# Four masked graph layers on one core: the attention-head stage splits the next quad's scores in two halves, one graph apart

## The chip, the cores and the metric

The kernel runs on one core of one Trainium2 chip. The metric is the device time of one execution in microseconds (us), lower is better; the median of three runs stands for a kernel.

## The reference

64 graphs of 128 nodes with 128 features pass four layers, each behind a layer norm and a ReLU and each added to its input. The change touches only the third, an attention with 8 heads:

```python
h = input @ W                                   # per graph: 128 nodes x 128 features
s1 = einsum('bif,hf->bhi', h, a1); s2 = einsum('bjf,hf->bhj', h, a2)
e = leaky_relu(s1[:, :, :, None] + s2[:, :, None, :] + a_b[None, :, None, None])
att = softmax(where(adj[:, None, :, :] > 0, e, NEG_INF), axis=-1)
h_prime = einsum('bhij,bjf->bif', att, h) / 8   # mean over the 8 heads
```

## The kernel before

The four layers are four stages, one after the other; the whole of `x` stays in on-chip memory. The stage of the heads (`phase_heads`) runs from about 640 to 960 us. It works on 16 quads of 4 graphs. Each engine runs an instruction list of its own, and every quad is cut into four **slots**, `i` = 0 to 3, one per graph. The slots are a software pipeline: in the slot of graph n the engines work on graphs n to n-4. Semaphores order the engines; the order within an engine is that of the code. The first quad and the last four stand written out, the others run in a loop of two quads per turn (`graphs`).

For graph n the work goes as follows. A slot number is that in which the step is issued, counted from the graph's own slot.

- TensorE, slot 0: four matmuls write the masked scores of 8 heads to `psE` (L955, L957). ScalarE copies them with a ReLU (L1018), also in slot 0.
- VectorE, slot 1: finishes the leaky ReLU in `eu` (L1068) and takes the maximum per head (L1072, "the maximum").
- ScalarE, slot 2: eight exponentials (L1012), which need that maximum.
- VectorE, slot 3: the reciprocal of the sums (L1059). GpSimd, slot 3: scales the exponentials by it (L918). TensorE, slot 3: 16 instructions of L977 turn and add up the heads in `psA`.
- VectorE, slot 4: copies `psA` to `attT` (L1064). TensorE, slot 4: multiplies by `h` (L965).

On VectorE one slot is therefore the reciprocal L1059, the copy L1064, then L1068 and L1072. On TensorE it is the scores L955/L957, L965, one job for the next quad, and L977.

The jobs for the next quad g+1 are spread over the slots of quad g. In slot 0 TensorE turns the inputs (L935) and ScalarE applies the ReLU (L996). In slot 1 TensorE forms the small score rows in `psF` (L940), and VectorE, behind that slot's maximum, splits them into three bf16 parts (`split_scores`): L1035 writes part 0, L1037 the rest in float32, L1040 part 1, L1042 part 2. SyncE waits for L1042 (L894), sends the parts to DRAM with two DMAs (L896), waits for both, and fetches them back in another layout with two DMAs (`lhs` at L900, `rhs` at L901). The semaphore `placed` tells TensorE that they are there; it waits for it ahead of L955 in slot 0 of quad g+1. In slot 3 TensorE writes `h` of quad g+1 over `psF` (L945), once L1037 is done, and ScalarE copies it (L1001). In slot 3 VectorE also adds the finished quad to `x` (L1047) and takes its layer-norm statistics (L264).

Of the kernel before, what the change touches and what calls it, by code (L numbers as in the profile page):

```python
# [40 lines left out]
def done(n):  # L41
    return n + 1 + BIAS
# [218 lines left out]
def ln_stats(nc, k, g):  # L261

    for i in range(G):
        nc.vector.bn_stats(k.stats[:, bass.ds(g * G + i, 1), :], k.x[:, bass.ds((g * G + i) * C, C)])  # L264
# [575 lines left out]
def phase_heads(nc, k):  # L840
# [6 lines left out]
    with ExitStack() as ctx:  # L847
# [26 lines left out]
        def graphs(eng, slot):  # L874


            def quad(g, p, first=False, tail=False, left=2):
                for i in range(G):
                    slot(g, p, i, lambda lag: (not first or i >= lag) and (not tail or i < lag), lambda l: l <= left)
            quad(0, 0, first=True)  # L880
            with eng.Fori(0, QUADS // 2 - 2) as t:
                for u in (0, 1):
                    quad(2 * t + (u + 1), 1 - u)
            quad(QUADS - 3, 1)
            quad(QUADS - 2, 0, left=1)
            quad(QUADS - 1, 1, left=0)
            quad(QUADS, 0, tail=True, left=0)

        with nc.Block() as block:
            @block.sync  # L890
            def _(sp):
                for g in range(QUADS):
                    p = g % 2
                    sp.wait_ge(s_split, done(4 * g + 3))  # L894
                    for half, first in ((0, 0), (1, S2)):
                        sp.dma_start(bounce[p, half].rearrange("t h c -> h t c"), parts[first:first + HEADS, p, :, :]).then_inc(bounced, 16)  # L896
                    sp.wait_ge(bounced, 32 * (g + 1))
                    if g >= 2:
                        sp.wait_ge(e_mm, done(g * G - (G + 1)))
                    sp.dma_start(lhs[0:ROWS, p, :], bounce[p, 0].rearrange("t h c -> (t h) c")).then_inc(placed, 16)  # L900
                    sp.dma_start(rhs[ROWS:KR, p, :, :], bounce[p, 1]).then_inc(placed, 16)  # L901
                    sp.wait_ge(placed, 32 * (g + 1))
# [124 lines left out]
            @block.vector  # L1027
            def _(dve):
                for s in (s_split, leaky, negmax, recip, att_ready, added):
                    dve.sem_inc(s, BIAS)  # L1030
                def split_scores(g, p, placed_before=True):
                    dve.wait_ge(s_mm, done(g))
                    if placed_before:
                        dve.wait_ge(placed, 32 * g - 32)
                    nc.vector.tensor_scalar(parts[:, p, 0, :], psF[0:SR, :], ab[:, 0:1], None, ALU.add).then_inc(s_split, 1)  # L1035
                    dve.wait_ge(s_split, done(4 * g))
                    nc.vector.scalar_tensor_tensor(out=rest[:, :], in0=psF[0:SR, :], scalar=ab[:, 0:1], in1=parts[:, p, 0, :],  # L1037
                                                   op0=ALU.add, op1=ALU.subtract).then_inc(s_split, 1)
                    dve.wait_ge(s_split, done(4 * g + 1))
                    nc.vector.tensor_copy(parts[:, p, 1, :], rest[:, :]).then_inc(s_split, 1)  # L1040
                    dve.wait_ge(s_split, done(4 * g + 2))
                    nc.vector.tensor_tensor(parts[:, p, 2, :], rest[:, :], parts[:, p, 1, :], ALU.subtract).then_inc(s_split, 1)  # L1042

                def finish(g):
                    dve.wait_ge(out_mm, done(g * G + (G - 1)))
                    xs = k.x[:, bass.ds(g * QC, QC)]
                    nc.vector.tensor_tensor(xs, psO[:, :], xs, ALU.add).then_inc(added, 1)  # L1047
                    dve.wait_ge(added, done(g))
                    ln_stats(nc, k, g)

                def slot(g, p, i, behind, ahead):
                    n = g * G + i
                    odd, even = (i - 1) % 2, i % 2
                    if behind(3):
                        m = n - 3
                        dve.wait_ge(expd, done(m))
                        at = (i - 3) % G
                        dve.wait_ge(scaled, done(m - G))
                        nc.vector.reciprocal(rz[:, at, :], zs[:, at, :]).then_inc(recip, 1)  # L1059
                    if behind(4):  # L1060
                        m = n - 4
                        dve.wait_ge(att_mm, done(m))
                        dve.wait_ge(out_mm, done(m - 2))
                        nc.vector.tensor_scalar(attT[:, even, :], psA[:, 0:N], 1.0 / HEADS, None, ALU.mult).then_inc(att_ready, 1)  # L1064
                    if behind(1):
                        m = n - 1
                        dve.wait_ge(e_copied, done(m))
                        nc.vector.scalar_tensor_tensor(out=eu[:, odd, :], in0=psE[:, odd, :], scalar=0.01, in1=eu[:, odd, :],  # L1068
                                                       op0=ALU.mult, op1=ALU.add).then_inc(leaky, 1)
                        dve.wait_ge(leaky, done(m))  # L1070
                        dve.wait_ge(expd, done(m - 2))
                        nc.vector.tensor_reduce(nmx[:, odd, :], eu[:, odd, :].rearrange("n (h j) -> n h j", j=N), AX.X, ALU.max,  # L1072
                                                negate=True).then_inc(negmax, 1)
                    if i == 1 and ahead(1):
                        split_scores(g + 1, 1 - p)
                    if i == 3 and behind(4):
                        finish(g - 1)
                split_scores(0, 0, placed_before=False)
                graphs(dve, slot)


# [791 lines left out]
```

## Time and profile before

| | before |
|---|---|
| median of three runs | 2086.39 us (2083.98 to 2087.57) |
| the profiled execution: its own time, its span | 2077.1 us, 2075.3 us |
| busy share of the span: TensorE, VectorE, ScalarE, GpSimd | 84%, 83%, 67%, 29% |
| mean granted TensorE clock | 0.945 of full speed |
| stage of the heads, 640 to 960 us: TensorE, VectorE, ScalarE, GpSimd busy | 286.1, 238.0, 281.7, 149.5 us of 320 |

The profile is one execution of its own. "PE" is TensorE's matmuls, "PEld" its weight loads, "DVE" VectorE, "ACT" ScalarE, "POOL" GpSimd, "SPq" SyncE's queue. The shares over the whole span mix four stages with different limits; only the last line of the table is about the stage of the change.

### The profile page before, as it was taken

The page shows a single profiled execution, that of the slowest core. Times are in us where ns is not written, and L with a number is a line of the kernel's source. Part 1 is how long each engine was busy: PE and PEld are TensorE (multiplying, and loading weights), DVE is VectorE, ACT ScalarE, POOL GpSimd, SP SyncE. Part 2 cuts the span into 40 slices and gives each one's busy share as a digit, 9 for nine tenths or more (in the row PEclk, how much of TensorE's full clock was granted, in tenths as well). Part 3 has the DMA queues.
Part 4 walks back from the last instruction along what each step waited for, and adds up shares of the span by engine and source line. Part 5 has one row for each costly group of instructions (what it writes and reads, how often), then busy time and mean ns, then how long its engine had stood idle before and what let it go on. Part 6 is the DMA issues. An engine that isn't in the chain of part 4 may idle for free. (4 is left out here: it accounts for less than half of the span.)

```text
span 2075.3 us, 43855 instructions
## 1 busy us (share of the span) xinstructions
PE 1737.3 (84%) x13771; PEld 1096.7 (53%) x13771; DVE 1727.0 (83%) x2689; ACT 1390.1 (67%) x3229; POOL 597.2 (29%) x449
## 2 busy tenths in 40 slices
PE   2966777777776899897799999999999678988886
PEld 1855556555663666665465555555555234444445
DVE  5878888888875777785799999999999577888887
ACT  0533333333334999895588888888888687888884
POOL 1530000000002544443344444444444211111110
PEclk9989998999887999997999999999999899999999
DMA  6000000000000000000055555555555699999993
GB/s 183 1 13 1 1 0 0 0 0 0 0 1 4 7 6 4 6 6 21 32 224 223 222 222 223 220 223 220 223 220 223 256 371 350 391 376 369 375 342 88
DMA packets 123567, 292.98 MB, mean 141 GB/s; under 512 B 21376, under 2 KB 57608, under 8 KB 123288
## 3 DMA queue, kind: packets, MB, share of 16 engines
q1 hardware_dynamic: 106360, 283.37, 35.9%
q10 hardware_dynamic: 16896, 8.39, 1.4%
q8 instruction: 26, 0.43, 0.1%
q0 software_dynamic: 256, 0.56, 0.1%
q14 instruction: 29, 0.24, 0.0%
HBM read 150.45 MB, written 141.82 MB: 141 GB/s over the span
## 5 line engine op out<-in xcount | busy, mean ns | idle before, releaser
L1316 POOL TENSOR_TENSOR pair_ring<-hd 128x2048 f32 (+1 forms) x64 | 269.5, 4211 | 310.1 <-DVE pair_ring L1341 310.1
L1401 ACT ACTIVATE v_hid<-v_psW 128x1024 f32<-128x1024 f32 x256 | 263.2, 1028 | 84.9 <-PE v_psW L1439 84.9
L771 DVE TENSOR_REDUCE m_part<-m_psS 128x128 f32<-128x2048 f32 (+1 forms) x128 | 258.9, 2023 | 66.1 <-PE m_psS L638 66.1
L1337 DVE TENSOR_TENSOR pair_ring<-v_psX,hd 128x2048 f32<-128x2048 f32 x128 | 292.3, 2289 | 17.1 <-PE v_psW L1439 17.1
L1439 PE MATMUL v_psW<-pair_ring,p_w1T 128*64 128x512 f32 x1024 | 288.5, 596 | 0.0
L1404 ACT ACTIVATE v_junk<-v_psW 128x1024 bf16<-128x1024 f32 x256 | 263.0, 1027 | 0.0
L638 PE MATMUL m_psS<-m_onehot,m_tableT 32*128 32x128 f32 x3584 | 151.8, 307 | 127.7 <-DVE m_part L771 123.4
L1439 PE MATMUL v_psW<-pair_ring,l_w1T 128*64 128x512 f32 (+1 forms) x1024 | 252.5, 587 | 0.0
L1430 PE MATMUL v_psW<-p_ends,v_weights 128*64 128x512 bf16 x1536 | 235.2, 381 | 3.1 <-DMA v_fold<-in_c_fold_dram 3.1
L638 PEld LDWEIGHTS m_psS<-m_onehot,m_tableT 32*128 32x128 f32 x3584 | 128.6, 207 | 147.3 <-issue 78.2
L708 ACT ACTIVATE m_tableT<-m_psTT 128x512 f32<-128x512 f32 (+1 forms) x128 | 69.3, 541 | 202.4 <-PE m_psTT L620 202.1
L1012 ACT ACTIVATE a_ex<-a_eu,a_nmx 128x128 f32<-128x128 f32 x512 | 197.6, 390 | 7.7 <-DVE a_rz L1059 7.3
L1587 DVE SCALAR_TENSOR_TENSOR pair_ring<-pair_ring 128x1024 f32<-128x1024 f32 x128 | 158.3, 1241 | 42.9 <-ACT pair_ring L1654 42.3
L1654 ACT ACTIVATE pair_ring<-pair_ring,p_beta,p_alpha 128x1024 f32<-128x1024 f32 x128 | 151.9, 1234 | 58.6 <-DMA pair_ring<-pair_hidden 56.9
L1430 PEld LDWEIGHTS v_psW<-p_ends,v_weights 128*64 128x64 bf16 x1536 | 129.9, 110 | 99.6 <-issue 34.1
L1439 PEld LDWEIGHTS v_psW<-pair_ring,l_w1T 128*64 128x64 f32 x1024 | 111.5, 137 | 110.0 <-issue 92.3
L918 POOL TENSOR_TENSOR a_ex<-a_ex,a_rz 128x1024 f32<-128x1024 f32 x64 | 121.3, 1896 | 166.1 <-DVE a_rz L1059 166.1
L977 PE MATMUL a_psA<-ident,a_ex 128*128 128x128 f32 x1024 | 142.7, 298 | 27.0 <-POOL a_ex L918 26.7
L977 PEld LDWEIGHTS a_psA<-ident,a_ex 128*128 128x128 f32 x1024 | 132.0, 209 | 45.1 <-POOL a_ex L918 33.5
L1341 DVE TENSOR_SCALAR pair_ring<-pair_ring 128x2048 int32<-128x2048 int32 x128 | 150.6, 1220 | 0.0
L1439 PEld LDWEIGHTS v_psW<-pair_ring,p_w1T 128*64 128x64 f32 x1024 | 109.5, 137 | 72.9 <-issue 58.1
L1346 DVE TENSOR_TENSOR pair_ring<-v_psX,hd 128x2048 f32<-128x2048 f32 x64 | 146.0, 2282 | 0.0
(260 smaller groups left out, 3354.9 us busy)
## 6 DMA issues: line engine op xcount, KB each, us to landing
pair_hidden<-v_hid SPq DMA_DIRECT2D x256, 512.0 KB, 2.6
pair_ring<-pair_hidden SPq DMA_DIRECT2D x128, 1024.0 KB, 7.7
adj_ring<-in_adj_dram ACTq DMA_DIRECT2D x16, 256.0 KB, 5.5
x_all<-in_x_dram ACTq DMA_DIRECT2D x16, 256.0 KB, 5.5
out_dram<-x_all SPq DMA_DIRECT2D x16, 256.0 KB, 2.3
pair_scores<-s_rot SPq DMA_DIRECT2D x64, 32.0 KB, 4.6
s_fwd<-pair_scores SPq DMA_DIRECT2D x64, 32.0 KB, 3.9
s_wide<-pair_scores SPq DMA_DIRECT2D x64, 32.0 KB, 5.0
```

Source lines behind the costliest of these rows:

```text
L638: last = nc.tensor.matmul(psS[:, q, b(c % 4)], tableT[rows, par, c % 4, :], onehot[rows, par, c % 4, :], start=True, stop=True)
L771: nc.vector.tensor_reduce(part[:, i % 2, r, :], psS[:, :, 0:w].rearrange("z q (c i) -> z i q c", i=N), AX.XY, ALU.max).then_inc(reduced, 1)
L977: last = nc.tensor.matmul(psA[:, 0:N], ex[:, (i - 3) % G, b(h)], k.ident[:, :], start=h == 0, stop=h == HEADS - 1)
L1012: last = nc.scalar.activation(ex[:, at, b(h)], eu[:, i % 2, b(h)], ACT.Exp, bias=nmx[:, i % 2, h:h + 1], accum_out=zs[:, at, h:h + 1])
L1316: nc.gpsimd.tensor_tensor(D[:, home(u, SLABS - 1), :].rearrange("c (h d i) -> c h d i", h=2, i=N), one, far, ALU.subtract).then_inc(psub_d ...
L1337: nc.vector.tensor_tensor(slab(s), own, windows(hd, n, s)[1], ALU.max).then_inc(max_done, 1)
L1401: nc.scalar.activation(hid[:, s, :], psW[:, buf, :], ACT.Identity, accum_out=hsum[:, bass.ds(m, 1)]).then_inc(evacuated, 1)
L1404: nc.scalar.activation(junk[:, at % 2, :], psW[:, buf, :], ACT.Square, accum_out=hsq[:, bass.ds(m, 1)]).then_inc(squared, 1)
L1430: nc.tensor.matmul(psW[half * HID:half * HID + HID, buf, c:c + 512], weights[:, u % 3, t * HID:(t + 1) * HID], ends[:, col:col + 512], sta ...
L1439: last = nc.tensor.matmul(psW[half * HID:half * HID + HID, buf, c:c + w], product[:, :], D[:, home(u, s), half * HALF + c:half * HALF + c ...
L1587: nc.vector.scalar_tensor_tensor(out=affined[:, s - 2, :], in0=affined[:, s - 2, :], scalar=0.01, in1=affined[:, s - 2, :], op0=ALU.mult, ...
L1654: nc.scalar.activation(affined[:, s - 2, :], h[:, slot(p, s), s % 2, :], ACT.Identity, bias=beta[:, 0:1], scale=alpha[:, 0:1]).then_inc(af ...
```

## The change

The last two of the four split instructions, with the waits in front of them, move into a function of their own that is called one slot later: behind the third graph's slot instead of the second's. No instruction is added or removed, and the first quad's split, ahead of the pipeline, still runs in one piece.

```diff
@@ split_scores
                     dve.wait_ge(s_split, done(4 * g))
                     nc.vector.scalar_tensor_tensor(out=rest[:, :], in0=psF[0:SR, :], scalar=ab[:, 0:1], in1=parts[:, p, 0, :],
                                                    op0=ALU.add, op1=ALU.subtract).then_inc(s_split, 1)
+
+                def split_rest(g, p):
                     dve.wait_ge(s_split, done(4 * g + 1))
                     nc.vector.tensor_copy(parts[:, p, 1, :], rest[:, :]).then_inc(s_split, 1)
                     dve.wait_ge(s_split, done(4 * g + 2))
@@ slot
                     if i == 1 and ahead(1):
                         split_scores(g + 1, 1 - p)
+                    if i == 2 and ahead(1):
+                        split_rest(g + 1, 1 - p)
                     if i == 3 and behind(4):
                         finish(g - 1)
                 split_scores(0, 0, placed_before=False)
+                split_rest(0, 0)
                 graphs(dve, slot)
```

## Rows read from the trace of the kernel before

**Rows 1.** Busy time of PE, PEld, DVE, ACT, POOL in 11 quads, then PEclk, DMA

```profile
686.88:900.93 214.05, 194.07 (x1126) 136.85 (x1125) 164.93 (x275) 193.46 (x771) 105.95 (x67) 0.94 0.03 5
```

**Rows 2.** Waits of ScalarE from 700 to 920 us, in total, times, longest

```profile
ACT a_eu L1018 <- PE a_psE L957: 8.5, 8, 1.1
ACT a_ex L1012 <- DVE a_rz L1059: 6.9, 10, 1.0
ACT a_h L1001 <- PE a_psF L945: 1.4, 8, 0.2
```

**Rows 3.** Timeline of ScalarE: start, duration; L996 stands once in each quad

```profile
686.88 0.59 ACT L996 ACTIVATE a_hT<-a_psF 128x512 f32<-128x512 f32 x1
...
900.93 0.59 ACT L996 ACTIVATE a_hT<-a_psF 128x512 f32<-128x512 f32 x1
...
918.78 0.59 ACT L996 ACTIVATE a_hT<-a_psF 128x512 f32<-128x512 f32 x1
```

**Rows 4.** Timeline of VectorE from slot 1 of one quad to slot 1 of the next

```profile
765.83 0.29 DVE L1064 TENSOR_SCALAR a_attT<-a_psA 128x128 f32<-128x128 f32 x1 [1.35 <-PE a_psA L977]
...
769.97 0.42 DVE L1040 CAST a_parts<-a_rest 40x512 bf16<-40x512 f32 x1
...
770.42 0.68 DVE L1042 TENSOR_TENSOR a_parts<-a_rest,a_parts 40x512 bf16<-40x512 f32 x1
...
771.03 0.19 DVE L1059 RECIPROCAL a_rz<-a_zs 128x8 f32<-128x8 f32 x1
...
772.54 1.22 DVE L1072 TENSOR_REDUCE a_nmx<-a_eu 128x8 f32<-128x1024 f32 x1
...
775.34 0.29 DVE L1064 TENSOR_SCALAR a_attT<-a_psA 128x128 f32<-128x128 f32 x1 [1.47 <-PE a_psA L977]
...
780.10 0.20 DVE L1059 RECIPROCAL a_rz<-a_zs 128x8 f32<-128x8 f32 x1 [0.31 <-issue]
...
784.51 0.29 DVE L1064 TENSOR_SCALAR a_attT<-a_psA 128x128 f32<-128x128 f32 x1 [1.43 <-PE a_psA L977]
```

**Rows 5.** Timeline of the other engines in the same quad

```profile
768.12 2.05 PE L977 MATMUL a_psA<-ident,a_ex 128*128 128x128 f32 x16
...
771.30 1.90 POOL L918 TENSOR_TENSOR a_ex<-a_ex,a_rz 128x1024 f32<-128x1024 f32 x1 [2.64 <-DVE a_rz L1059]
...
772.53 1.02 ACT L1018 ACTIVATE a_eu<-a_psE 128x1024 f32<-128x1024 f32 x1
...
773.25 2.05 PE L977 MATMUL a_psA<-ident,a_ex 128*128 128x128 f32 x16 [1.33 <-POOL a_ex L918]
...
773.93 0.40 ACT L1012 ACTIVATE a_ex<-a_eu,a_nmx 128x128 f32<-128x128 f32 x1 [0.38 <-DVE a_rz L1059]
...
782.33 2.05 PE L977 MATMUL a_psA<-ident,a_ex 128*128 128x128 f32 x16 [0.70 <-POOL a_ex L918]
```

**Rows 6.** The next quad: timeline, and one stretch of busy times (columns as in rows 1)

```profile
791.92 3.68 PE L977 MATMUL a_psA<-ident,a_ex 128*128 128x128 f32 x16 [1.33 <-POOL a_ex L918]
...
796.92 1.02 ACT L1018 ACTIVATE a_eu<-a_psE 128x1024 f32<-128x1024 f32 x1 [1.13 <-PE a_psE L957]
...
793.00:794.00 1.00, 1.00 (x7) 1.00 (x6) 0.00 (x0) 1.00 (x7) 1.00 (x1) 0.50 0.14 38
```

**Rows 7.** Timeline: the way of the parts through DRAM, and who takes them

```profile
771.18 0.62 SPq L896 DMA_DIRECT2D head_scores<-a_parts  x2
...
773.35 0.30 SPq L900 DMA_DIRECT2D a_lhs<-head_scores  x1
...
773.69 0.28 SPq L901 DMA_DIRECT2D a_rhs<-head_scores  x1
...
779.41 0.38 PE L955 MATMUL a_psE<-a_rhs,a_lhs 27*128 27x512 bf16 x1
...
890.57 0.28 SPq L901 DMA_DIRECT2D a_rhs<-head_scores  x1
...
893.11 0.10 PEld L955 LDWEIGHTS a_psE<-a_rhs,a_lhs 27*128 27x128 bf16 x1 [0.23 <-DMA a_rhs<-head_scores]
```

## The prediction

> **What bounds the kernel now.** Three of the four stages are untouched, so I read the stage of the heads alone, and in it the 11 quads from one L996 (686.88 us) to the twelfth (900.93 us), because ScalarE issues L996 once per quad. They took 214.05 us, 19.46 each, and ScalarE was busy for 193.46 of it, the most of any engine next to TensorE, whose modelled busy time is 194.07 [rows 1]. The last full quad, 900.93 to 918.78, took only 17.85 [rows 3]. ScalarE had no wait in it, so 17.85 is the length of its own work for a quad. The 11 quads at that pace would take 196.35; 17.7 us more went somewhere.
>
> The list of ScalarE's waits says where: 6.9 us in ten waits ahead of the exponentials (L1012), 8.5 us in eight ahead of the PSUM copy (L1018), 1.4 us ahead of L1001, 16.8 together [rows 2]. The first names the reciprocal L1059, and that is not what the exponentials wait for. In the timeline they start at 773.93 [rows 5], while the maximum L1072 runs from 772.54 to 773.76 [rows 4]; it is that maximum, 0.17 earlier, which they need. The reciprocal merely overlaps its end. The code agrees: L1012 waits for the maximum of the same graph, and its wait on a reciprocal is for one four graphs older.
>
> Why is the maximum late? The timeline of VectorE, followed with GpSimd and TensorE, shows a ring that closes once per quad [rows 4, 5]:
> - L1064 at 765.83 (slot 1) to the reciprocal of slot 2 at 771.03: 5.20 us, VectorE alone (L1064, L1068, L1072, the four split instructions).
> - Reciprocal 771.03, GpSimd 771.30, TensorE's L977 773.25, and L1064 of slot 3 at 775.34: 4.31 us, in which VectorE waits 1.47.
> - L1064 775.34 to the reciprocal of the next slot 0 at 780.10: 4.76 us, VectorE alone.
> - Again over GpSimd and TensorE to L1064 at 784.51: 4.41 us, with 1.43 of waiting.
>
> The sum is 18.68 us. It is longer than ScalarE's 17.85, so the ring sets the pace here and ScalarE waits. In this quad the four split instructions are inside the first leg, ahead of the reciprocal that starts the second. That turn has the loop's own 0.31 us of "issue" in it [rows 4], so one without it needs about 18.3.
>
> The other 8.5 us come from TensorE's clock. In the next quad the 16 instructions of L977 in slot 2 take 3.68 us instead of 2.05, and the granted clock is 0.50, the lower of the two levels (1.2 GHz) [rows 5, 6]. TensorE had stood 1.33 us for GpSimd immediately before. ScalarE's copy L1018 then waits 1.13 [rows 6]; eight such waits are in the list [rows 2]. The waits of slot 0, 0.70 us [rows 5], are followed by full clock.
>
> **The change, part by part.** Nothing is added or dropped. L1040 and L1042, with their gaps, take from 769.97 to 771.10: 1.13 us [rows 4]. Nothing moves on other engines by code, only the instant at which SyncE is released. I replay the quad of rows 4, 5 and 7 in its own clock.
>
> 1. *Slot 2 starts earlier.* L1037 ends just before 769.97. The reciprocal of slot 2, at 771.03 before, starts about 769.90, and GpSimd at 770.17 instead of 771.30. TensorE's L977 starts 772.12 instead of 773.25. TensorE was free at 771.92 before (773.25 less 1.33) and is so no later now; L965 of this slot, which had to follow VectorE's L1064, comes earlier too. Its wait of 1.33 shrinks to between 0.2 and 0.8 us; I take 0.5.
> 2. *A small part comes back.* VectorE's L1064 of slot 2 needs L977 of slot 1, which runs 768.12 to 770.17 [rows 5], so it starts 770.22, up to 0.32 behind the reciprocal. From reciprocal to maximum it was 1.51 (771.03 to 772.54), so the maximum now starts 771.73 at the latest and ends 772.95 instead of 773.76. The exponentials could start 773.12; ScalarE is free at 773.55 (L1018 from 772.53, 1.02 long) [rows 5]. The 0.38 wait is gone with 0.43 to spare.
> 3. *Where the 1.13 goes.* L1040 now follows that maximum, at about 772.88 (neighbours overlap by under 0.1), and L1042 ends 774.01, the reciprocal of slot 3 overlapping it. L1064 of slot 3 can start only after L977 of slot 2, so at 774.21 (772.12 and the 2.09 between 773.25 and 775.34). The pair thus lies in what was the 1.47 wait [rows 4], with the next reciprocal in it too, and under 0.2 left. If that cover were gone, it would cost up to 1.13 per quad, that is, the old time.
> 4. *The ring.* 18.68 less 1.13 is 17.55 for a turn with the loop's jump, and about 17.15 without. Both are under ScalarE's 17.85, so ScalarE becomes the bound, and one isolated slow-clock stretch (about 1.6 us, 3.68 against 2.05) can be caught up again.
> 5. *The transfer.* This is what the change makes late. The queue behind it is SyncE's alone: L894, two DMAs, a wait, L900 and L901. SyncE has nothing else. L1042's end moves from 771.10 to 774.01, so the first DMA from 771.18 to 774.09. The first leg takes 2.17 (771.18 to 773.35). When the second lands no row of this quad shows: if it is as long as the first, 4.34 after 771.18; the one landing that shows as a releaser is at 893.11, 2.54 after its issue at 890.57, which makes 5.05 [rows 7]. I keep both: `placed` at 778.43 to 779.14. TensorE takes it at L955 in slot 0 of the next quad, at 779.41 before [rows 7], and 1.13 earlier now, 778.28. So TensorE waits 0.2 to 0.9 us there. Behind it stand L965, L935 and L977. From L955 to where L977 could start is 2.2 us of TensorE work (779.41 to 782.33 less its wait of 0.70) [rows 5, 7], thus 780.6 to 781.4; GpSimd releases that L977 at 782.33 less 1.13, 781.20. The wait falls into the one for GpSimd, to within 0.2. I take no cost, and 0.2 per quad (2.2 us) as its upper bound. If the cover is gone, TensorE's lateness goes on to L1064 and the ring, one for one.
> 6. *h of the next quad.* L945 waits for L1037, which has not moved. The 0.18 waits at L1001 follow TensorE's slot 3, which comes 1.13 earlier; they go.
>
> **The sum.** By ScalarE's pace 17.7 us (214.05 less 196.35), by its listed waits 16.8. I take the middle, 17.2. The profiled execution ran 2077.1 us (span 2075.3, 1.8 around it), and its counterpart should read about 2060. The median of the runs is 2086.4, 9.3 above the profiled one, a difference the trace doesn't explain; taken off the median, the gain gives 2069.2, and I say 2069.
>
> **The rivals.**
> - *The slow clock stays.* The waits of TensorE shrink from 1.33 to 0.5 in slot 2, but slot 0 now holds two short ones close together (0.2 to 0.9 for `placed`, then GpSimd). If the clock still falls in eight of eleven quads, each adds about 1.6 to the ring: 17.35 on average and 8/11 of 1.6 make 18.5 a quad, 19.46 less 18.5 by 11 is 10.5 us. That gives about 2076. For it speaks that we see drops wherever waiting is densest; against it that the 0.70 waits of slot 0 cost none. The Trainium skill, TensorE: Matmul & The Clock Gate, in "A second HAM failure mode: psum-queue depth-cycling", says that frequent micro-idles between groups of matmuls are enough to make the clock swing between its levels; by that rule the 0.5 and 0.7 us waits that remain keep it swinging, and the time would be this rival's, 2076, rather than 2069. The trace so far shows swings only behind the 1.33 waits. 0.17.
> - *The stall only moves.* VectorE's cover in slot 3 is under 0.2 us. If the pair doesn't fit beside GpSimd and TensorE (each of the handovers longer than replayed), the ring stays near 18.3 to 18.7 plus clock drops: within 4 us of 2086. For it: 2.1 us of handovers in the sum are short hops each read once. Against: the total of VectorE is 164.93 in 214.05 [rows 1], 15.0 of 19.46 per quad. 0.09.
> - *Slower: the parts arrive too late.* The way through DRAM stands on the ring in slot 0. It decides from a landing after about 779.0 (step 5); each microsecond beyond adds up to one per quad once the ring's 0.4 us of room is used, and a wait of over 1.3 there would also be where the clock falls. With legs 2.5 us longer than replayed, 2.5 less 0.4 by 14 quads is 29 us on top of 2069: about 2098. For it: the slack at L955 falls from 3.2 to 3.9 us (779.41 less 776.23 or 775.52) to less than none. Against: such a lateness is over twice the spread between my two bounds. 0.05.
>
> **How the numbers follow.** The main case has 0.69: between 14 us (some drops left, 0.2 a quad for `placed`) and 19, thus 2067 to 2072, and 2065 to 2074 with the 2 us by which the runs of before stray from their median. The range must hold the clock rival too, 2072 to 2080: 2064 to 2081. Outside lie the moved stall and the slower case, 0.14, and a little at each end. A measurement of this kernel can tell about 0.2%, 4 us, from no change. Main case and clock rival are both faster by more, 0.86; no change 0.08, slower 0.06.
>
> **What would show it.** Right: L996 comes every 17.85 to 18.0 us through the loop; no wait of L1012 behind L1059 or L1072; L1040 behind the third maximum, with L1064 of slot 3 still waiting a little for L977; TensorE's wait ahead of slot 2's L977 near 0.5; few or no stretches at clock 0.50 between 686 and 900; L955 of slot 0 within 0.9 us of the end of slot 3's L977. Wrong: L996 still at 18.3 or more without a slow clock (the ring has another leg than I followed), L977 in slot 0 or 2 at 3 us and more (clock), or L955 of slot 0 waiting a microsecond or more for the DMA of `rhs`.

## The result, and the profile after

The changed kernel took 2058.41 us in the median of four runs (2051.86 to 2060.79); the kernel before took 2085.18 in four. The ratio on record is 0.9886, 95% interval 0.985 to 0.9922; it is not the quotient of the two medians, which is 0.9872. So the changed kernel is faster by 26.8 us in the medians, and by 16 to 31 by the interval. I had forecast 2069, 2064 to 2081: the direction was right, the time lies 5.6 us below the range. The traced execution took 2060.8 us (span 2059.0), 16.3 less than that of before.

Most lines of the file behind the edit are two higher in the profiles after: the reciprocal is L1061, the copy L1066, the leaky ReLU L1070, the maximum L1074, the second half of the split L1042 and L1044.

Timeline of ScalarE in the changed kernel, the answer to [rows 3] (12 starts, first and last shown), and the busy times between them (PE, PEld, DVE, ACT, POOL, then clock), the answer to [rows 1, 6]:

```profile
690.55 0.59 ACT L996 ACTIVATE a_hT<-a_psF 128x512 f32<-128x512 f32 x1
...
885.46 0.59 ACT L996 ACTIVATE a_hT<-a_psF 128x512 f32<-128x512 f32 x1
```

```profile
690.55:885.46 194.91, 179.65 (x1126) 127.06 (x1124) 167.77 (x276) 190.88 (x772) 105.85 (x67) 1.00 0.03 6
```

The 11 quads took 194.91 us, 17.72 each (before 214.05, 19.46 [rows 1]), with the same instructions. ScalarE is busy for 98% of it, the granted clock is 1.00 instead of 0.94, and the list of ScalarE's waits is empty from 700 to 920 us, where three entries with 16.8 us stood [rows 2]. TensorE's busy time fell by 14.4 us, as nothing in this stretch ran at the lower clock any more.

The timeline of one quad, all engines, the answer to [rows 4, 5 and 7]:

```profile
767.61 2.05 PE L977 MATMUL a_psA<-ident,a_ex 128*128 128x128 f32 x16 [0.50 <-POOL a_ex L918]
...
768.63 0.41 DVE L1042 CAST a_parts<-a_rest 40x512 bf16<-40x512 f32 x1
...
769.08 0.68 DVE L1044 TENSOR_TENSOR a_parts<-a_rest,a_parts 40x512 bf16<-40x512 f32 x1
...
769.83 0.62 SPq L896 DMA_DIRECT2D head_scores<-a_parts  x2
...
770.43 1.23 DVE L1070 SCALAR_TENSOR_TENSOR a_eu<-a_psE,a_eu 128x1024 f32<-128x1024 f32 x1 [0.40 <-ACT a_eu L1018]
...
772.00 0.30 SPq L900 DMA_DIRECT2D a_lhs<-head_scores  x1
...
772.34 0.28 SPq L901 DMA_DIRECT2D a_rhs<-head_scores  x1
...
774.94 0.38 PE L955 MATMUL a_psE<-a_rhs,a_lhs 27*128 27x512 bf16 x1 [0.99 <-DMA a_rhs<-head_scores]
...
777.22 2.05 PE L977 MATMUL a_psA<-ident,a_ex 128*128 128x128 f32 x16 [0.28 <-POOL a_ex L918]
...
779.40 0.29 DVE L1066 TENSOR_SCALAR a_attT<-a_psA 128x128 f32<-128x128 f32 x1 [1.03 <-PE a_psA L977]
```

The first row is slot 2: TensorE's wait for GpSimd is 0.50 where it was 1.33. The pair of the split lies behind it, and the 1.47 us in which VectorE waited for L977 ahead of slot 3 are gone; VectorE now waits 0.40 for **ScalarE's** copy there. The cost that I had looked for stands at L955: TensorE waits 0.99 us for the parts and starts 2.6 us after the issue of `rhs`. Then it waits another 0.28 for GpSimd, so in this quad the transfer is hidden by just that.

This quad has the longest of these waits. Over the 13 quads of each trace from the third L996 on they are 0.44 to 0.99 us in the first and 0.44 to 0.86 in the second. The wait for GpSimd that follows is at most 0.64, and in 10 of the 26 quads none is listed: there TensorE and GpSimd come at about the same time, and nothing is left to spare. The quads take 17.71 or 17.72 even so.

**What the totals can tell.** I traced both kernels a second time (below) and cut each trace at the first L996 and at ScalarE's table load that ends the stage of the heads:

| trace | whole span | stage of the heads | 13 quads, third L996 to last | slow stretches in them (granted clock 0.50) |
|---|---|---|---|---|
| before | 2075.3 | 324.1 | 249.8 | 8 |
| before, second trace | 2076.8 | 324.4 | 249.9 | 8 |
| after | 2059.0 | 304.2 | 230.3 | 0 |
| after, second trace | 2050.1 | 304.0 | 230.3 | 0 |

The stage repeats to 0.3 us: the change takes 20.1 us off it (means of the two pairs: 324.25 and 304.1). The span doesn't repeat: 8.9 us lie between two traces of the changed kernel. They lie outside this stage: the span less the stage is 1751.2 and 1752.4 us in the two traces of before, 1754.8 and 1746.1 in those of after. In further runs of the kernel before, 29 on one chip had a median of 2080.36, and all but one, a slow one, lay between 2061 and 2092 us.

The table leaves out the quads at the ends. Every kernel here also has a slow stretch ahead of its third L996. The changed kernel has one more that the kernel before lacks, in both traces, in the quad behind the last L996, where TensorE has no job for a next quad; the waits just ahead of it are 0.66 for the parts and 0.36 for GpSimd:

```profile
919.00:922.00 3.00, 3.00 (x14) 2.34 (x13) 0.70 (x3) 2.91 (x13) 1.82 (x1) 0.50 0.00 0
```

What it costs is inside the 304 us of the stage. I therefore judge the experiments by the stage in their traces, and by totals only where several runs stand behind them.

### The profile page after: what moved, and what is told of

Read it like the earlier page. It is cut to its first block and busy times, and to the rows that moved or that the text cites. A ratio compares the mean times of both kernels' runs of the same rounds, so it can differ in the third digit from the quotient of the medians.

```text
span 2059.0 us, 43855 instructions
## 1 busy us (share of the span) xinstructions
PE 1728.3 (84%) x13771; PEld 1091.8 (53%) x13771; DVE 1731.7 (84%) x2689; ACT 1387.9 (67%) x3229; POOL 591.4 (29%) x449
## 5 line engine op out<-in xcount | busy, mean ns | idle before, releaser
L1342 DVE TENSOR_TENSOR pair_ring<-v_psX,hd 128x2048 f32<-128x2048 f32 x128 | 292.4, 2289 | 17.6 <-PE v_psW L1444 17.5
L977 PE MATMUL a_psA<-ident,a_ex 128*128 128x128 f32 x1024 | 134.1, 286 | 12.7 <-POOL a_ex L918 12.4
L977 PEld LDWEIGHTS a_psA<-ident,a_ex 128*128 128x128 f32 x1024 | 123.0, 197 | 30.8 <-POOL a_ex L918 19.8
```

Source lines behind the costliest of these rows:

```text
L977: last = nc.tensor.matmul(psA[:, 0:N], ex[:, (i - 3) % G, b(h)], k.ident[:, :], start=h == 0, stop=h == HEADS - 1)
L1342: nc.vector.tensor_tensor(slab(s), own, windows(hd, n, s)[1], ALU.max).then_inc(max_done, 1)
```

## The experiments

**Both kernels again.** No edit.

> The kernel before, unchanged, for a second trace of it. The median of before is about 2085 us, its traced execution took 2077.1; the change was worth 26.8 us in the medians and 16.3 in the two traces. If the traced execution of before was a lucky one, with fewer slow-clock stretches of TensorE in the stage of the heads than usual (8 of them between 669 and 919 us), a second trace shows more of them (12 or so) and a stage longer than 324.1 us, by 1.5 us for each. If instead the untouched stages make the difference, the stage of the heads is again 324 us and the rest of the span is longer by some 8 us.

> The changed kernel once more. Its median should be 2056 to 2061 us, ratio 0.986 to 0.989. In the trace L996 comes every 17.7 us from the third quad on and ScalarE waits for nobody; if the first trace was typical, the slow-clock stretches are 0 or 1 between the third quad and the fifteenth. If the clock only happened to stay high there, this trace shows some drops.

Before: 2079.46 us in the median of 12 runs, ratio 1.0004 (0.9966 to 1.0041), stage 324.4, again 8 slow stretches. After: 2052.5 in 6 runs (2038.95 to 2068.7, and 2056 to 2061 was expected of the median), ratio 0.9899 (0.9845 to 0.9953), stage 304.0, none. So the first trace of before was not a lucky one in this stage; that idea fell. What varies lies elsewhere. Two answers for the tile of the attention weights in the fourth layer (64 instructions, first to last start), from the first traces of before and of after, and one from the second trace of after:

```profile
L1613 DVE TENSOR_SCALAR s_dg<-ident,s_rz x64: 285/286/289, 1684.0 to 2038.6; 128x128 f32<-128x128 f32 x64
```

```profile
L1618 DVE TENSOR_SCALAR s_dg<-ident,s_rz x64: 285/287/288, 1665.4 to 2022.3; 128x128 f32<-128x128 f32 x64
```

```profile
L1618 DVE TENSOR_SCALAR s_dg<-ident,s_rz x64: 285/286/289, 1665.9 to 2013.3; 128x128 f32<-128x128 f32 x64
```

That untouched stretch takes 354.6, 356.9 and 347.4 us; over the traces of this document it took from 342 to 365, with no relation to the edits. In the experiments below, a kernel that ran only once is therefore read by its stage alone.

**The clock alone: four more matmuls in TensorE's wait.**

```diff
+        psW = k.ps(ctx, "a_psW", [N, QC])
...
+                    if i == 2:
+                        for _ in range(4):
+                            nc.tensor.matmul(psW[:, :], k.identb[:, :], k.negm[:, 0:QC], start=True, stop=True)
                     if behind(3):
```

> The kernel before with four more matmuls (128x512, bf16, into a PSUM bank of their own) on TensorE in slot 2 of every quad, ahead of L977, in the 1.33 us that it stands there; VectorE's order is untouched. Ring theory: a quad without a slow clock still takes 18.3 to 18.7 us, because the split is still in the ring, but the eight slow stretches of about 1.5 us go: 9 to 15 us faster than before, and ScalarE still waits 0.4 to 0.9 us a quad ahead of the exponentials. Clock theory (the change gained by the clock alone): all of the gain, 25 us or more. If the slow clock isn't caused by that wait: no change, 2085.

Stage 313.8 us, no slow stretch in the 13 quads, 2071.93 in 12 runs, ratio 0.9971 (0.9942 to 1.0). TensorE in slot 2, and ScalarE's L996 (L1000 here) in four quads of the trace:

```profile
779.68 1.03 PE L975 MATMUL a_psW<-negm,identb 128*128 128x512 bf16 x4
...
781.18 2.05 PE L981 MATMUL a_psA<-ident,a_ex 128*128 128x128 f32 x16 [0.47 <-POOL a_ex L919]
```

```profile
716.80 0.59 ACT L1000 ACTIVATE a_hT<-a_psF 128x512 f32<-128x512 f32 x1
735.51 0.59 ACT L1000 ACTIVATE a_hT<-a_psF 128x512 f32<-128x512 f32 x1
753.78 0.59 ACT L1000 ACTIVATE a_hT<-a_psF 128x512 f32<-128x512 f32 x1
772.47 0.59 ACT L1000 ACTIVATE a_hT<-a_psF 128x512 f32<-128x512 f32 x1
```

```profile
ACT a_ex L1016 <- DVE a_rz L1063: 6.9, 11, 0.9
```

The quads alternate 18.71, 18.27, 18.69: the two lengths of the ring that I had read, with and without the loop's jump. ScalarE still waits for the maximum in all of 11 quads. So of the change's 20.1 us, taken in this order, 10.4 are the clock (324.25 less 313.8) and 9.7 the ring (313.8 less 304.1). Neither theory alone has the whole. That it is the wait of TensorE which brings the clock down is shown by this kernel: VectorE's order and ScalarE's wait are those of before, only 1.03 us of matmuls are put into TensorE's wait in slot 2, where 0.47 of waiting is left.

**The ring shortened elsewhere.** The split in one piece, the statistics of a quad one slot later than before, in slot 0 behind the maximum. One more quad stands written out ahead of the loop for it, which the cut below does not show.

```diff
+                def stats(g):
                     dve.wait_ge(added, done(g))
                     ln_stats(nc, k, g)
...
+                    if i == 0 and behind(2 * G):
+                        stats(g - 2)
                     if i == 3 and behind(4):
                         finish(g - 1)
```

> The kernel before, the split in one piece as before, but the layer-norm statistics (L264, 1.2 us of VectorE with its wait) taken out of slot 3 and done one slot later, behind the maximum of slot 0; for this one more quad is written out ahead of the loop. Ring theory: another 1.2 us leaves a leg of the ring in which VectorE works alone, for a leg with 1.4 us of waiting; a quad falls from 18.3 to 18.7 to ScalarE's 17.7 to 17.9, and the gain is nearly that of the change: 15 to 27 us faster. TensorE's wait of 1.3 us in slot 2 stays, so slow-clock stretches may stay too, and then 10 to 15. If only the place of the split matters (SyncE's release, the wait in slot 2), no gain.

Stage 308.8 us, 2057.32 in 12 runs, ratio 0.9929 (0.9892 to 0.9966): 15.4 us of stage without touching the split. Seven of the 13 quads took 17.71 or 17.72 us. Four slow stretches stayed, each behind the wait that is still there in slot 2:

```profile
804.33 3.09 PE L977 MATMUL a_psA<-ident,a_ex 128*128 128x128 f32 x16 [1.33 <-POOL a_ex L918]
```

Two of them no longer cost 1.5 us but 0.6 (quads of 18.3), as the ring had room. The waits of 0.5 to 0.7 us in slot 0 are gone in this kernel and the slow stretches are four instead of eight; what those short waits add to the long one was not separated.

**The pair of VectorE once more, in two places.** A dummy pair of the same shapes on scratch tiles, in slot 1 or in slot 0.

```diff
+                    if i == 1 and ahead(1):     # i == 0 in the second kernel
+                        nc.vector.tensor_copy(junkb[:, 0, :], junk[:, :])
+                        nc.vector.tensor_tensor(junkb[:, 1, :], junk[:, :], junkb[:, 1, :], ALU.subtract)
                     if i == 1 and ahead(1):
                         split_scores(g + 1, 1 - p)
```

> The changed kernel with a dummy pair in slot 1, ahead of the split: a copy and a subtraction on scratch tiles of the same shape as L1042 and L1044, 1.1 us of VectorE. It restores the length of the ring and leaves SyncE's release and the second half where the change put them. Ring theory: a quad back at 18.3 to 18.7 us in the untroubled case, and TensorE's wait in slot 2 back at about 1.3, so the slow clock comes back too: stage of the heads 314 (if the clock stays) to 324 us (if it falls as before) instead of 304. Rival (it was the order of the split that mattered, or the clock by itself): 304 to 307 us.

> The changed kernel with the dummy pair (1.1 us of VectorE) in slot 0 instead of slot 1, where it made the stage 319 us. Ring theory: in slot 0 it lies beside GpSimd and TensorE, in the 1.03 us that VectorE waits ahead of L1066 in the next slot, so at most 0.1 to 0.3 us a quad gets through and ScalarE has that much room: stage 304 to 307 us, no slow clock. If VectorE's amount of work counts and not its place: 319 us again.

In slot 1 (2086.2 us in one run): stage 319.3 us, six slow stretches, and the waits of before are back (from 700 to 900 us):

```profile
PE a_psA L980 <- POOL a_ex L921: 17.9, 19, 1.3
...
ACT a_eu L1021 <- PE a_psE L960: 5.4, 5, 1.1
ACT a_ex L1015 <- DVE a_nmx L1077: 4.9, 10, 0.7
```

In slot 0 (2064.8 us in one run): stage 304.3, every quad 17.70 to 17.72, no slow stretch. The same 1.1 us of VectorE cost 15 us in one slot and nothing in the other. What decides is the place, not VectorE's amount of work. In the kernel with the pair in slot 1 the wait ahead of the exponentials names the maximum (L1077), and not the reciprocal as the list of before did.

**The transfer.** One more DMA leg of SyncE, and then the second half of the split one slot later again.

```diff
+                    sp.wait_ge(bounced, 48 * g + 32)
+                    sp.dma_start(spare[:, :], wl_copy[:, :]).then_inc(bounced, 16)
+                    sp.wait_ge(bounced, 48 * (g + 1))
-                    sp.wait_ge(bounced, 32 * (g + 1))
```

```diff
-                    if i == 2 and ahead(1):
+                    if i == 3 and ahead(1):
                         split_rest(g + 1, 1 - p)
```

> The changed kernel with a third DMA leg in SyncE's way of the parts: between the write of the parts and their fetch it also copies a 128x128 tile to DRAM and waits for it, 2.2 us more until the parts are placed (values unchanged). In the trace of the changed kernel TensorE already waits 0.99 us for them in slot 0 and then 0.28 for GpSimd; VectorE waits 1.03 in the next slot and the ring has 0.2 to 0.5 us of room. So about 0.3 us of the 2.2 is hidden by GpSimd's wait and 0.4 by the ring's room: 1.5 us a quad, stage 304 plus 14 times 1.5, 325 us, perhaps with slow-clock stretches on top in slot 0. Rival (the way through DRAM has room): 304 to 308.

> The second half of the split one slot later again, behind the maximum of slot 3. The first half is still out of it. L1044 ends about 4.2 us later, so the parts are placed 4.2 us later than in the changed kernel, where TensorE already waits about 1 us: 3.5 us or more per quad, a quad of 21 us and a stage of 350 us, slower than before. If the transfer had room, about 304 to 310.

With the leg: stage 335.9 us (325 expected), quads mostly of 19.1 to 20.4, ten slow stretches, and 2082.9 us in one run. One slot later: the stage, from the first L996 at 644.03 to the table load at 1038.26, is 394.2 us (350 expected), a quad 23.9, fourteen slow stretches, and 2141.5 us in one run. Waits for the parts in the one and in the other, 700 to 900 us:

```profile
PE a_psE L959 <- DMA a_rhs<-head_scores: 17.6, 8, 2.9
ACT a_eu L1022 <- PE a_psE L961: 15.1, 16, 2.5
```

```profile
ACT a_eu L1018 <- PE a_psE L957: 45.4, 18, 4.6
PE a_psE L955 <- DMA a_rhs<-head_scores: 36.1, 8, 4.7
```

The slower rival's mechanism is real, and the price of being late was even higher than I wrote down. At least part of that is the clock: the slow stretches now begin in slot 0, around TensorE's wait there (2 us and longer with the leg, 4.7 one slot later), while no wait of 1.33 is left in slot 2; how much is the clock was not separated. Both cost more stage (31.8 and 90.1 us) than the change brings. The change stops one step short of that.

**Is ScalarE the bound now?** The changed kernel with the statistics in slot 0 as well; then ScalarE's copy L1018 cut to half its columns, without and with that. In the kernels with the cut, half of `eu` lacks its ReLU term, and GpSimd sets `eu` to zero once, ahead of the stage.

```diff
-                        nc.scalar.activation(eu[:, i % 2, :], psE[:, i % 2, :], ACT.Relu, scale=0.99).then_inc(e_copied, 1)
+                        nc.scalar.activation(eu[:, i % 2, 0:HC // 2], psE[:, i % 2, 0:HC // 2], ACT.Relu, scale=0.99).then_inc(e_copied, 1)
```

> The changed kernel with the statistics L264 moved to slot 0 as well. The ring is then 1.2 us shorter still, 16.2 us. If ScalarE is the bound of the changed kernel, a quad stays at 17.7 us and the stage at 304 us, and VectorE's waits grow. If the ring is still the bound, or half of it, the quad falls towards 16.5 and the stage towards 290.

> The changed kernel with ScalarE's PSUM copy L1018 cut to half its columns (the other half of eu is left without its ReLU term), 0.43 us less in each of four graphs: ScalarE's own quad is then 16.0 us. If ScalarE alone bounds the changed kernel, the quad falls to 16.0 and the stage by 24 us. By the ring I replayed it stops at 17.15 to 17.55, and the way of the parts through DRAM closes a ring of its own of about 17.6 (from VectorE's slot 1 to L1044 7.9, to the landing 5.2, TensorE 2.2, L977 and its hop 2.2, 0.2): quad 17.3 to 17.6, stage 299 to 303.

> The same cut of ScalarE's copy, on the changed kernel with the statistics moved to slot 0 too. VectorE's ring is then 16.2 us, ScalarE 16.0, TensorE's own work 16.3. If the transfer closes a ring of 17.6, the quad is the same as with the cut alone, 17.3 to 17.6; if not, it falls to 16.3 to 16.6 and the stage to 285.

The statistics alone change nothing in the quads: the 13 take 230.3 us to the tenth, stage 305.1 (2069.9 us in one run), and VectorE waits for ScalarE in 40 slots instead of 12 (700 to 900 us):

```profile
DVE a_eu L1072 <- ACT a_eu L1018: 15.1, 40, 0.5
```

This kernel also has the quad written out ahead of the loop, so that is not what shortened the stage in the kernel with the split in one piece.

With ScalarE's cut the quads fall to between 17.0 and 17.5 (13 of them in 224.25 us, stage 295.2, 2064.9 us in one run), and ScalarE waits for the maximum again (700 to 880 us). Not 16.0: there is the ring. A pair of quads takes 34.6 or 34.7, where the 17.15 and 17.55 of the prediction make 34.7; where the two lengths stand bare they are 17.10 and 17.51, and in other pairs both are 17.3. The stage is shorter than the 299 to 303 that I expected.

```profile
ACT a_ex L1015 <- DVE a_nmx L1077: 8.5, 20, 0.5
```

With both, 220.5 us for the 13, 16.96 each, stage 289.4, 2045.7 us in one run. That is neither the 17.3 to 17.6 which I expected from a ring over the transfer nor the 16.3 to 16.6 of engines alone. So my transfer ring of 17.6 was reckoned at least 0.6 too long; what sets 16.96 I did not separate (TensorE waits up to 0.7 for the parts, ScalarE up to 0.5 for the maximum).

**A version with a shorter stage than both.** The statistics in slot 0, and the copy of `h` (L1001) by VectorE in slot 3.

```diff
-                        nc.scalar.activation(hs[:, p, :], psF[:, :], ACT.Copy).then_inc(h_ready, 1)
+                    nc.vector.tensor_copy(hs[:, p, :], psF[:, :]).then_inc(h_ready, 1)     # VectorE, i == 3, ahead of finish
```

> An attempt at a faster kernel: the changed one with the statistics in slot 0, and the copy of h (L1001, 0.59 us a quad) taken from ScalarE and done by VectorE in slot 3. ScalarE's quad is then 17.1 us and VectorE's ring about 17.0. If these were all, 0.6 us a quad less than the changed kernel, 8 to 9 us of stage (295). With the transfer's ring at 17.6 only 0.1 to 0.2 a quad, stage 301 to 303 us: no measurable difference to the changed kernel, 1.0 to 1.4% faster than the kernel before.

2051.77 us in the median of 6 runs, ratio to before 0.9829 (0.9776 to 0.9881). The stage is 297.9 us, 6.2 less than the changed kernel's, between the two values that I expected (295, or 301 to 303). Each quad in the loop takes 17.23:

```profile
738.41 0.59 ACT L996 ACTIVATE a_hT<-a_psF 128x512 f32<-128x512 f32 x1
755.64 0.59 ACT L996 ACTIVATE a_hT<-a_psF 128x512 f32<-128x512 f32 x1
772.87 0.59 ACT L996 ACTIVATE a_hT<-a_psF 128x512 f32<-128x512 f32 x1
```

17.72 less 17.23 is 0.49, what L1001 (0.59 long, overlapping its neighbours) costs in ScalarE's sequence. ScalarE is still the bound: from 700 to 900 us no wait of it is listed, and it is busy for 185.25 us of the 189.28 from 704.22 to 893.50. The transfer does not hold the kernel at 17.6. In the totals this kernel can't be told from the changed one; in the stage it can.

## Why the prediction was right in direction and outside its range

- **The bound.** Right, and confirmed twice over: the ring's 18.27 and 18.69 us stand bare in the kernel with a warm clock, and about 17.1 and 17.5 in that with the short copy.
- **What the exponentials wait for.** Right: the maximum, though the list named the reciprocal.
- **"ScalarE had no wait in it, so 17.85 is the length of its own work".** Wrong by 0.13 us. The list doesn't show waits that short. Two copies L1018 with neither L996 nor L1001 between them start 4.33 us apart once in that quad (908.86 to 913.19) and 4.18 or 4.19 otherwise. Its own work is 17.72. Over 11 quads that is 1.4 us.
- **Steps 1 to 4.** Right in kind. TensorE's wait in slot 2 fell to 0.41 to 0.50 (I took 0.5). The slow stretches in the 13 quads fell from eight to none; the main case had left some in at its slow end. "ScalarE becomes the bound" holds.
- **Step 5, the transfer.** TensorE waits 0.44 to 0.99 us for the parts; I had 0.2 to 0.9. GpSimd covers most of it, and in the quads in which it doesn't, the ring's room does: 17.72 in all of them. No cost, as taken. The slack was read too short afterwards, in the expected 17.6 of a transfer ring.
- **The sum.** 17.2 us against 20.1 in the stage. Of the 2.9 missing, 1.4 are the 17.85. 0.5 is "I take the middle" between 17.7 and 16.8. The list was read from 700 to 920 us and held against 686.88 to 900.93; over that very stretch it adds up to 17.2 (8.5, 7.3 and 1.4), and still lacks the short waits. The last 1.0 are the quads and ends outside my eleven, which I left out (324.1 to 304.2 is 19.9 in the first pair of traces, of which the 11 quads have 19.1). The list's split into 6.9 us for the maximum and 8.5 for the clock came out as 9.7 and 10.4.
- **The step that failed is the one from the traced execution to the median and its range**: "2065 to 2074 with the 2 us by which the runs of before stray from their median". Three runs within 3.6 us were taken for the spread of the kernel. Its runs reach over 30 us, 2061 to 2092. I had the sign of it in hand, as the traced execution was 9.3 us below the median, and passed over it. The forecast of 2069.2 missed by 10.8 us. 2.9 of them are the stage (20.1 instead of 17.2); with that alone put right the forecast is 2066.3, inside the range. 1.2 are the median of before, 2085.2 with the fourth run instead of 2086.4. The other 6.7 have no place in the traces, where the span less the stage is 1751.8 us before and 1750.5 after, in the means of the two; they are within the spread of the runs, and no run shows more of their cause. The interval, 16 to 31 us, holds 20.1 as well as 17.2.
- **Luck.** "About 2060" for the traced execution came true, 2060.8, but the stage fell by 19.9 us there, not 17.2, and the untouched rest was 3.6 us longer than in the trace of before.
- **The rivals.** The slow clock that stays: wrong for the 13 quads, where the remaining waits of up to 0.64 us in GpSimd's name and 0.44 to 0.99 for the parts brought no drop in either trace; the one stretch that came new, behind the last L996, is in a quad with less work for TensorE. The Trainium skill, TensorE: Matmul & The Clock Gate, "A second HAM failure mode: psum-queue depth-cycling", has frequent micro-idles swing the clock in one kernel. For the waits of 0.4 to 1.0 us that recur in these 13 quads the runs don't agree, with 0 stretches in both traces, and the measurement decides. The moved stall: wrong, VectorE now waits for ScalarE. Slower by the transfer: not reached, but one leg more or one slot later reaches it.

## What to carry to other kernels

Follow the cross-engine ring of a software pipeline once around and mark each leg as "one engine alone" or "waiting for another": work moved from the first kind to the second is free up to the wait, and the same work can cost all or nothing by its slot. Then compare the ring with the busiest engine's own sequence; the gain ends there, and before trusting a gain look at what the moved step releases last, here a transfer with between nothing and 0.6 us to spare. Judge a change in one stage by that stage's length in two traces, and take the spread of the total from many runs, not three.

## What the runs showed of the hardware that I had not expected

- Filling a recurring 1.33 us wait of TensorE with 1.03 us of matmuls into an unused bank removed all eight stretches at the lower clock (granted 0.50), worth 10.4 us of stage; the same wait left in place, with a shorter ring, still brought four. In the changed kernel a wait of 0.44 to 0.99 us in slot 0 of every quad, beside waits of 0.4 to 0.5 in slot 2, brought none in the 13 quads.
- The stage of the heads repeats to 0.3 us between executions, while an untouched, transfer-heavy stretch of the fourth layer takes anything from 342 to 365 us.
